# A four-part transformer layer on one core: narrower square sums, a reordered table tree, and a last group without next-weight work

## The reference, cut to what matters

```python
# x: 128 sequences x 32 tokens x 512 channels
h   = mixed(x, cond_128)                        # per-sequence 32x32 mix over tokens
proj = einsum('bld,pd->blp', h, in_proj_w)      # gate, conv input (x, B, C), dt
xBC = silu(conv1d(hbc, taps=4))                 # causal, along the 32 tokens
...                                             # 64 heads of 64, 8 groups: y_t = state_t . C_t
y   = y + x * D
var = mean(yg * yg, axis=-1)                    # over the 512 channels of a group
yn  = yg * rsqrt(var + EPS) * norm_weight * silu(gate)
x   = x + einsum('bli,di->bld', yn, out_proj_w)
z   = conv2(x) + context                        # second half of the layer
e   = norm(z, axis=-1);  mask = e > 64
x   = x + where(mask, z @ W8.T, z @ W4.T) + bias
# W8: 8-bit codes looked up in a table of 256 values per output row; W4: 4-bit codes, 16 values
```

## Time and profile before

| what | value |
|---|---|
| median of the runs | 3560.12 us |
| the profiled execution, its own time | 3564.81 us |
| its span, first to last instruction | 3563.1 us |
| TensorE busy | 3478.4 us (98%) |
| VectorE busy | 3082.2 us (87%) |
| ScalarE busy | 1459.6 us (41%) |
| GpSimd busy | 477.3 us (13%) |
| mean granted TensorE clock | 0.993 |

### The profile page before, as it was taken

One profiled execution on the slowest core, in us unless ns is written; L12 is line 12 of the kernel. 1 busy time (PEld: TensorE's weight loads), 2 busy tenths in 40 slices (PEclk: granted clock), 3 DMA queues, 4 the chain that ended last, 5 costly groups with the idle time before them and its releaser, 6 DMA issues. The chain is left out here.

```text
span 3563.1 us, 58721 instructions
## 1 busy us (share of the span) xinstructions
PE 3478.4 (98%) x19789; PEld 2874.5 (81%) x19789; DVE 3082.2 (87%) x4843; ACT 1459.6 (41%) x2218; POOL 477.3 (13%) x334
## 2 busy tenths in 40 slices
PE   6699999999999999999999999999999999999999
PEld 4488888888888888888888888888888888888888
DVE  6589999999999999999999999999999999998443
ACT  3444444444444444444444444444444444444111
POOL 3201111011111011111011111011111011110333
PEclk9799999999999999999999999999999999999999
DMA  7722335332533353333533363334433363335331
GB/s 235 264 101 105 119 142 184 116 129 106 200 130 116 114 189 130 118 129 117 195 129 108 116 212 118 111 129 162 145 129 118 112 212 109 115 129 161 100 93 57
DMA packets 220673, 490.29 MB, mean 138 GB/s; under 512 B 39595, under 2 KB 85067, under 8 KB 211043
## 3 DMA queue, kind: packets, MB, share of 16 engines
q1 hardware_dynamic: 216964, 488.88, 39.3%
q0 software_dynamic: 304, 0.82, 0.1%
q10 hardware_dynamic: 3376, 0.26, 0.1%
HBM read 320.51 MB, written 169.39 MB: 137 GB/s over the span
## 5 line engine op out<-in xcount | busy, mean ns | idle before, releaser
L837 PE MATMUL p_cv<-ht,wt 128*128 128x512 f32 x5376 | 1298.6, 394 | 4.4 <-DMA ht<-h_d 4.4
L837 PEld LDWEIGHTS p_cv<-ht,wt 128*128 128x128 f32 x5376 | 1000.7, 188 | 230.2 <-issue 15.6
L932 PE MATMUL bank<-wot,gy 128*128 128x512 f32 x3072 | 737.4, 396 | 0.0
L932 PEld LDWEIGHTS bank<-wot,gy 128*128 128x128 f32 x3072 | 567.3, 188 | 128.1 <-issue 11.0
L982 ACT ACTIVATE xc<-p_cv,cvb,cvw 128x512 f32<-128x512 f32 x256 | 199.8, 780 | 933.4 <-PE p_cv L837 933.4
L1067 DVE SCALAR_TENSOR_TENSOR xc<-p_cv,cvw,xc 128x496 f32<-128x496 f32 (+2 forms) x768 | 545.2, 717 | 31.4 <-ACT xc L982 7.9
L837 PE MATMUL bank<-ht,wt 128*128 128x512 f32 x2304 | 562.0, 393 | 0.0
L837 PEld LDWEIGHTS bank<-ht,wt 128*128 128x128 f32 x2304 | 427.8, 188 | 87.9
L811 POOL TENSOR_TENSOR r<-rv,neg_half 128x4 f32<-128x4 f32 x64 | 90.0, 1407 | 2453.3 <-DVE rv L1155 2453.3
L1089 DVE TENSOR_TENSOR m<-cbm,y 128x1024 f32<-128x1024 f32 x256 | 301.6, 1220 | 7.8
L1067 DVE SCALAR_TENSOR_TENSOR xc<-bank,cvw,xc 128x496 f32<-128x496 f32 (+2 forms) x384 | 275.6, 718 | 33.4 <-ACT xc L982 21.7
(11 more groups left out here) (187 smaller groups left out, 3632.9 us busy)
## 6 DMA issues: line engine op xcount, KB each, us to landing
ht<-h_d SPq DMA_DIRECT2D x64, 2048.0 KB, 7.8
acc<-acc_d SPq DMA_DIRECT2D x64, 1024.0 KB, 7.4
wt_d<-wnext SPq DMA_DIRECT2D x128, 512.0 KB, 3.4
acc_d<-acc SPq DMA_DIRECT2D x64, 1024.0 KB, 4.3
wt<-wt_d SPq DMA_DIRECT2D x70, 512.0 KB, 8.4
stage<-in_L_attn_in_proj_w SPq DMA_DIRECT2D x106, 256.0 KB, 2.7
h_d<-ht_out SPq DMA_DIRECT2D x8, 2048.0 KB, 7.9
wot<-wt_d SPq DMA_DIRECT2D x28, 512.0 KB, 6.0
```

The source lines that it names most:

```text
L837: ins = pe.matmul(pb[:, :], wt[:, n, l, k, :], ht[:, rr, k, :], start=(q == 0 and k == 0), stop=(q == 2 and k == KC - 1))
L932: ins = pe.matmul(bank[OUT[t]][:, :], gy[:, c, l, t * P:(t + 1) * P], wot[:, rr, c, :], start=(c == 0 and q == 0), stop=(c == CT - 1 and q ...
```

## The change

1. `NSQ` goes from 128 to 2. The square-sum matmuls of stage 2 (L926) and stage 3 (L1332) stream two columns of ones and write two columns.
2. VectorE's second and third `add_squares` move ahead of more of the tree: the second goes between the first two joins, the third right behind the second of these joins, ahead of `pair(4)`, `pair(5)` and the join of la and lc. The counts that they wait for change with it, and the join of lb and ld now has a wait and an `s_w8go` increment.
3. In the last group no raw weights are loaded, turned, split or stored: on SP, TensorE, ScalarE and VectorE. The loops over g end one earlier, and the last group's 8 blocks have a loop of their own, on TensorE, ScalarE and VectorE (on VectorE its own copy inside the last of the four tile loops).

```diff
-NSQ = P
+NSQ = 2
@@ SP, step(g, j, last)
-                    nxt = g if last else g + 1
+                    nxt = g + 1
-                    load_raw(nxt, j)
+                    if not last:
+                        load_raw(nxt, j)
...
-                    sp.wait_ge(s_nlo, 2 * it + 2)
-                    for u, n in enumerate(next_chunks(j)):
-                        sp.dma_start(sh.wt_d[ds(g, 1), n]...
+                    if not last:
+                        sp.wait_ge(s_nlo, 2 * it + 2)
+                        for u, n in enumerate(next_chunks(j)):
+                            sp.dma_start(sh.wt_d[ds(g, 1), n]...
@@ PE, attend(g, j, prepare)
-                        for u in range(2):
+                    for u in range(2 if prepare else 0):
                         pe.wait_ge(s_raw[u], 16 * it + 16)
...
-                        pe.wait_ge(s_nlo, 2 * it + 2)
+                    if prepare:
+                        pe.wait_ge(s_nlo, 2 * it + 2)
...
+                with pe.Fori(0, G - 1) as g:
+                    with pe.Fori(0, NBLK) as j:
+                        attend(g, j, True)
+                with pe.Fori(0, NBLK) as j:
+                    attend(G - 1, j, False)
@@ ACT and DVE: the same split of the loops; range(2 if prepare else 0) around the next-weight work
@@ DVE, the tail
                     add_squares(1, 5)
                     low(CT - 1)
                     join(1, la, lb)
-                    join(1, lc, ld)
                     add_squares(2, 6)
+                    join(1, lc, ld)
+                    add_squares(3, 7)
                     pair(4, lb, 6)
                     pair(5, ld, 7)
                     join(2, la, lc)
-                    add_squares(3, 9)
-                    join(1, lb, ld)
+                    join(1, lb, ld, 9)
                     pair(6, lc, 10)
                     pair(7, ld, 11)
```

More of the change, by code:

```diff
@@ L735, in step @@
                         sp.dma_start(sh.x2_0[:, :, :, :].rearrange("p t r m -> p t (r m)"), acc_v[0]).then_inc(sh.s_x2[0], 16)
-                    sp.wait_ge(s_nlo, 2 * it + 2)
-                    for u, n in enumerate(next_chunks(j)):
-                        sp.dma_start(sh.wt_d[ds(g, 1), n].rearrange("o p n -> p (o n)"),
-                                     wnext[:, u, :, :].rearrange("p a n -> p (a n)").bitcast(F32)).then_inc(s_nst, 16)
+                    if not last:
+                        sp.wait_ge(s_nlo, 2 * it + 2)
+                        for u, n in enumerate(next_chunks(j)):
+                            sp.dma_start(sh.wt_d[ds(g, 1), n].rearrange("o p n -> p (o n)"),
+                                         wnext[:, u, :, :].rearrange("p a n -> p (a n)").bitcast(F32)).then_inc(s_nst, 16)
                     sp.wait_ge(s_proj, NPJ * (it + 1))
@@ L777, in _ @@
                     step(G - 1, j, True)
-                sp.wait_ge(s_nst, 32 * NIT + 32)
+                sp.wait_ge(s_nst, 32 * NBLK * (G - 1) + 32)
             @block.gpsimd
@@ L827, in _ @@
                 pe.wait_ge(s_wlo, NWC)
-                with pe.Fori(0, G) as g:
-                    with pe.Fori(0, NBLK) as j:
[L830 to L851, removed]
-                                for u in range(2):
[L853 to L917, removed]
-                        pe.wait_ge(s_nlo, 2 * it + 2)
[L919 to L935, removed]
@@ new lines, in attend, with project, turn_x, scan @@
+                def attend(g, j, prepare):
+                    it = NBLK * g + j
+                    def project(n):
+                        pe.wait_ge(s_wt[n], 16 * g + 16)
+                        pb = bank[PROJ_BANK[n]]
+                        for q, (l, rr) in enumerate(PASSES):
+                            for k in range(KC):
+                                ins = pe.matmul(pb[:, :], wt[:, n, l, k, :], ht[:, rr, k, :],
+                                                start=(q == 0 and k == 0), stop=(q == 2 and k == KC - 1))
+                        ins.then_inc(s_proj, 1)
+                    def turn_x(t):
+                        for c in range(CT):
+                            ins = pe.transpose(bank[XT[t % 2]][:, c * P:(c + 1) * P], xc[:, 2 + c, t * P:(t + 1) * P], sh.ident[:, :])
+                        ins.then_inc(s_xt, 1)
+                    def scan(c):
+                        for t in range(TT):
+                            if c == 0:
+                                pe.wait_ge(s_dtx, TT * it + t + 1)
+                            for u in range(2):
+                                h = 2 * c + u
+                                ins = pe.matmul(bank[YB[c % 2]][u * HP:(u + 1) * HP, t * P:(t + 1) * P], dtx[:, t, h * HP:(h + 1) * HP],
+                                                m[:, h, t, :], start=True, stop=True)
+                        ins.then_inc(s_yp, 1)
+                    pe.wait_ge(s_ht, 16 * it + 16)
+                    for n in range(NCV):
+                        if n == 0:
+                            pe.wait_ge(s_z, CT * it + CT)
+                        elif n == 2:
+                            pe.wait_ge(s_acc, TT * it + 1)
+                        elif n >= 3:
+                            pe.wait_ge(s_conv, NCV * it + n - 2)
+                        project(n)
+                    pe.wait_ge(s_segr, 2 * it + 4)
+                    pe.wait_ge(s_acc, TT * it + TT)
+                    pe.wait_ge(s_y, CT * it + CT)
+                    for q in range(SEGB):
+                        for half in range(2):
+                            ins = pe.matmul(bank[SEG[q]][:, :], sh.mask_gtr[:, :],
+                                            segr[:, half, q * 2 * HG:(q + 1) * 2 * HG, :].rearrange("p h l -> p (h l)"),
+                                            start=(half == 0), stop=(half == 1))
+                        ins.then_inc(s_seg, 1)
+                    pe.wait_ge(s_conv, NCV * it + 4)
+                    project(NCV)
+                    pe.wait_ge(s_silu, NCV * it + 2)
+                    pe.wait_ge(s_rv, it + 1)
+                    for t in range(TT):
+                        ins = pe.matmul(bank[CB][:, t * P:(t + 1) * P], xc[:, 0, t * P:(t + 1) * P], xc[:, 1, t * P:(t + 1) * P],
+                                        start=True, stop=True)
+                    ins.then_inc(s_cb, 1)
+                    for c in (1, 2):
+                        pe.wait_ge(s_conv, NCV * it + 4 + c)
+                        project(NCV + c)
+                        for t in (2 * c - 2, 2 * c - 1):
+                            if c == 1:
+                                pe.wait_ge(s_silu, NCV * it + NCV)
+                            else:
+                                pe.wait_ge(s_dtx, TT * it + t - 1)
+                            turn_x(t)
+                    for u in range(2 if prepare else 0):
+                        pe.wait_ge(s_raw[u], 16 * it + 16)
+                        if u == 0:
+                            pe.wait_ge(s_exp, SEGB * it + 1)
+                        else:
+                            pe.wait_ge(s_z, CT * it + CT + 2)
+                        for k in range(KC):
+                            ins = pe.transpose(bank[NEXT[u]][:, k * P:(k + 1) * P], stage[u][:, k * P:(k + 1) * P], sh.ident[:, :])
+                        ins.then_inc(s_nps, 1)
+                    pe.wait_ge(s_cbm, it + 1)
+                    scan(0)
+                    pe.wait_ge(s_exp, SEGB * it + SEGB)
+                    scan(1)
+                    pe.wait_ge(s_z, CT * it + CT + 1)
+                    project(NCV + 3)
+                    for c in (2, 3):
+                        pe.wait_ge(s_y, CT * it + CT + c - 1)
+                        scan(c)
+                    pe.wait_ge(s_z, CT * it + CT + 3)
+                    if prepare:
+                        pe.wait_ge(s_nlo, 2 * it + 2)
+                    pe.wait_ge(s_dtx, TT * it + TT)
+                    pe.wait_ge(s_wot, 16 * KC * g + 16 * KC)
+                    for c in range(CT):
+                        if c == CT - 1:
+                            pe.wait_ge(s_y, CT * it + CT + 3)
+                            pe.wait_ge(s_sqsum, (CT - 1) * (it + 1))
+                            for t in range(TT):
+                                ins = pe.matmul(bank[SSQ][:, t * NSQ:(t + 1) * NSQ], y[:, 0, t * P:(t + 1) * P], sh.ones[:, 0:NSQ],
+                                                start=True, stop=True)
+                            ins.then_inc(s_ssq, 1)
+                        pe.wait_ge(s_ulo, CT * it + c + 1)
+                        for t in range(TT):
+                            for q, (l, rr) in enumerate(PASSES):
+                                ins = pe.matmul(bank[OUT[t]][:, :], gy[:, c, l, t * P:(t + 1) * P], wot[:, rr, c, :],
+                                                start=(c == 0 and q == 0), stop=(c == CT - 1 and q == 2))
+                            if c == CT - 1:
+                                ins.then_inc(s_out, 1)
@@ L1006, in _ @@
```

(9 more changed lines are left out.)

317 lines of the change are left out of this document (158 added, 159 removed).

## The result

The changed kernel takes 3524.35 us (median of 4 runs, 3522.6 to 3527.09) against 3559.89 before (4 runs). The ratio is 0.990, 95% interval 0.9885 to 0.9916: 35.5 us less. I had forecast 3494 with a range of 3480 to 3524. The direction was right, the size twice too large, and the time lies just above the range. The two signs of being wrong that the prediction named both came: the square sums keep 0.81 us, and a round stays at 48.01. The profiled execution had a span of 3523.0 us and 3524.74 us in all.

The account below looks back on a forecast made before the run. It took TensorE as the bound, busy 3478.4 of 3563.1 us, with VectorE close behind. Savings of 61 (rounds), 3 (last group) and 3.2 us (stage 3) made 67, taking 3560.1 to 3493, stated as 3494; range 3480 to 3524.

Parts of the forecast that it names:

- two signs of being wrong: Prediction called wrong if the square sums keep their 0.8 us, or if the round stays above 48 us.
- part 1: VectorE's tail: the new order removes TensorE's whole stall before the square sums, 0.60 us a round (0.46 to 0.70).
- the price of coming out of a scan: TensorE's matmuls behind a scan: up to 0.24 us of the apparent stall may be this and remain.
- part 2: Square sums on TensorE: streaming 2 columns instead of 128 saves 0.40 us a round, and 3.2 us in stage 3.
- Carried on to 2 columns: Square-sum pairs: extending the 64-column transposes' price saves 0.05 to 0.074 us a pair, 0.4 to 0.6 a round.
- by the sum: Round of 47.6 us, where TensorE's and VectorE's bounds meet: 0.95 us less in each of 64 rounds, 61 us.
- the 0.101 of the prediction: Square-sum pairs on TensorE: 0.101 us from start to start with 128 columns.
- columns don't pay: Square sums: the 128-wide fp32 weight load alone paces the pairs, so only 0.60 us a round; 3519 to 3528, chance 0.20.
- VectorE as the next bound: At `project(3)`, the first convolution comes late; as a rival 3510 us, or 3531 at 0.35 a wait, chance 0.12.
- the cycle: VectorE's chain from `project(3)` through y and `rv` to the first convolution: 47.14 us, 47.38 to 47.62 with the longer tail.
- The last group: Last 8 rounds: TensorE drops eight transposes, but scan 0 waits for the fourth dtx; 0.37 us a round, 3.0 in all.
- Stage 3 and the copies of the code: Two columns save 3.2 us in stage 3's 64 pairs; copied loops cost nothing, at most one 0.5 us wait.

Follow-up runs that it names:

- one square sum: The changed kernel with one square-sum matmul instead of four, all four token tiles taking the variance of the first; 3500.19 us, ratio 0.9827.
- the rounded sums: The changed kernel with square sums and ones in the long matmuls' rounded fp32 type, one load-and-matmul pair instead of two; 3490.15 us, ratio 0.9802.

## Why the prediction was wrong, step by step

- **The stall and the new order (part 1): the mechanism right, the size a little large.** I took 0.60 us from bounds of 0.46 and 0.70. A round lost 0.54: 0.46 in front of the square sums and 0.10 of their first load, less 0.02 in the matmuls behind them. The undisturbed 36 output matmuls take 8.35 us, not 8.21: 0.14 of the 0.24 that I had named as the price of coming out of a scan is real. The 0.06 too much makes 4 us in 64 rounds.
- **Two columns (part 2): this step failed.** "Carried on to 2 columns: 0.05 to 0.074 saved in a pair" came out at 0.00. Undone in the changed kernel and done alone in the kernel before, it moves the time by about 1 us, within the noise. This was 0.40 x 64 = 26 us (or 22 by the sum, which counted stall and columns together as 0.95 a round and not 1.00), and 3.2 more in stage 3. With 2, 64 or 128 streamed columns an fp32 pair with 128 stationary columns starts 0.112 us behind the one before; the 0.101 of the prediction was a mean that held the cheap first pair. With 64 stationary columns it is 0.058. What the pace of these matmuls follows is the columns of the stationary operand. That it is the loading of them which takes the time fits all of these runs, and no run shows it by itself.
- **Why the rows misled.** I used as the nearest row by shape. They are transposes, and in transposes fewer streamed columns do go with a faster pace. The four at 1806.75 in the earlier trace rows, which stream 128, take 1807.19 - 1806.75 = 0.44 us where the four dt transposes took 0.30:

```profile
1807.19 0.60 PE L905 MATMUL p_cv<-ident,stage 128*128 128x128 f32 x4
```

  By single starts it is 0.109 against 0.062 us, both with 128 stationary columns (the rows differ too, 128 against 64). With 128 streamed columns the two kinds lie close, 0.109 and 0.112, so that they looked like one price list. The list of TensorE's loads in the trace of before, by line and shape, has what I didn't read:

```profile
L844 PEld LDWEIGHTS bank<-ident,xc 128*128 128x128 f32 x1024 | 119.5, 140 | 16.5
...
L884 PEld LDWEIGHTS bank<-xc 128*128 128x128 f32 x512 | 66.9, 191 | 5.1
L926 PEld LDWEIGHTS bank<-ones,y 128*128 128x128 f32 x512 | 61.9, 191 | 45.0 <-DVE y L1139 45.0
```

  The mean load of a transpose is 140 ns, that of an fp32 matmul 191, at the same 128x128. That a shorter load is what lets a transpose's streamed columns show is my reading of it. The length of a load's record is not its pace: the dt transposes have loads of 139 ns and start 0.062 us apart, so successive loads overlap. The run with the transposes as matmuls shows only that, at one shape, the kind changes both the load's length and the pace.
- **The rival that came true** was "columns don't pay", with 0.20 and 3519 to 3528. Its rule in the Trainium skill (TensorE: Matmul & The Clock Gate, section LDWEIGHTS) gives an estimate of 107 ns for 128 columns. The trace agrees for fp32 matmuls, with 0.112 us. It does not for the dt transposes, which load 128 columns too and start 0.062 apart. I weighed the rule against this row of another kind and gave it too little.
- **VectorE as the next bound: right, but never reached.** The change stops at 48.01 us a round, above the cycle. The runs that shorten TensorE further meet the wait at `project(3)`: with one square sum it holds the round at 47.60 us, 0.17 above the sum, and with the rounded sums, where TensorE's own part of the cycle is shorter, it is met at 47.46 and costs little.
- **The last group: right.** 0.42 us a round for the predicted 0.37, by the mechanism named: the scan waits for the fourth dtx. 3.4 us against 3.0.
- **Stage 3 and the copies of the code:** nothing to be seen of the 3.2 for the columns, by the run with two columns alone. The copies brought no wait that the list shows; the end of stage 2 has one new wait of 0.47 us.

The sum of what was measured: 56 rounds at 0.54 and 8 at 0.96 make 38 us, less the 0.5 at the end, against 35.5 between the medians. The 2 us between them are within the interval of the ratio, which reaches from 30 to 41 us.

## What to carry to other kernels

Before narrowing what a short matmul streams, look at what paces it. In this kernel a dense run of small fp32 matmuls with 128 stationary columns goes at 0.112 us a pair whether 2, 64 or 128 columns are streamed, and only fewer pairs helped (the rounded type takes one pair instead of two), or fewer stationary columns. A reduction that another engine waits for belongs ahead of work that nobody waits for, even if it costs two waits of 0.14 us. The nearest row for a price must be of the same kind of instruction, not just of a similar shape. And a mean over a short group holds its first and last steps: take the price of one more from two groups of different length.

## What the runs showed that I had not expected

A group of matmuls that uses half the partitions or half the columns of the array, between full ones, kept TensorE's loads idle for 0.36 us in front of it. With half the partitions it made the round 0.27 us longer (1857.42 - 1809.14 = 48.28) than with all of them. A matmul of the rounded type with 2 streamed columns costs 0.11 us behind another one, as much as one of the two records of an fp32 matmul. And in the kernels with the rounded sums other groups of matmuls, which nobody had edited, got 0.14 us a round shorter, for a reason that stays open.
